# Four graph layers on one core: operands in PSUM, index arrays kept in SBUF, scans over eight features, gathers moved across stage ends, products on pairs of node tiles

## The reference

```
h = relu(layernorm(x)); x += segment_sum(h[src] * weight, dst) @ W0.T + b0
h = ...; per source node: sum, max and mean of edge_attr (32 features), and u
         x += relu([sum, max, mean, u] @ W1 + b1) @ W2 + b2
h = ...; hw[r] = h @ Wr[r] for 8 relations
         M = segment_sum(hw[etype, src] / degree[dst], dst)
         x += relu(0.2 h + 0.8 M)            (h where the degree is 0)
h = ...; e = leaky_relu(h[src] @ al + h[dst] @ ar); a = softmax of e over each dst
         x += elu(segment_sum(h[src] * a, dst))
```

## Time and profile before

| | us |
|---|---|
| device time, median of 3 runs | 24807.4 |
| lowest, highest | 24771.12, 24842.9 |
| span of the profiled execution | 21400.8 |
| POOL busy in the span | 16823.9 (79%) |
| DVE busy | 8437.1 (39%) |
| PE busy | 4183.5 (20%) |
| ACT busy | 2199.2 (10%) |

### The profile page before, as it was taken

The page is one execution under the profiler, slowest core; times in us unless marked ns, Lnnn a source line. Parts: engine busy times, 40 slices in busy tenths (PEclk is TensorE's granted clock), DMA queues, the critical chain, the costliest instruction groups (busy, mean ns, idle before and its releaser), DMA issues. The chain is left out here.

```text
span 21400.8 us, 135402 instructions
## 1 busy us (share of the span) xinstructions
PE 4183.5 (20%) x27708; PEld 3439.5 (16%) x27708; DVE 8437.1 (39%) x31691; ACT 2199.2 (10%) x10623; POOL 16823.9 (79%) x13464
## 2 busy tenths in 40 slices
PE   1111677777760000000061000000000000000000
PEld 1111566656650000000040000000000000000000
DVE  5555666666655455454431111111113222222223
ACT  0000444444440000000010000000000000000000
POOL 7888777777778888888856777777777787787777
PEclk9999755555555555555555555555555555555555
DMA  2111111111102222222221111111112111111112
GB/s 52 36 33 36 33 27 27 27 27 27 27 24 74 67 69 74 66 69 74 66 64 53 45 45 45 45 45 45 46 47 32 46 46 46 46 46 46 42 46 46
DMA packets 660027, 993.34 MB, mean 46 GB/s; under 512 B 393615, under 2 KB 447856, under 8 KB 629104
## 3 DMA queue, kind: packets, MB, share of 16 engines
q0 software_dynamic: 430432, 388.76, 9.6%
q10 hardware_dynamic: 28944, 432.98, 4.9%
q1 hardware_dynamic: 200192, 167.64, 2.9%
HBM read 466.94 MB, written 521.52 MB: 46 GB/s over the span
## 5 line engine op out<-in xcount | busy, mean ns | idle before, releaser
L338 POOL DMA_INDIRECT att_G<-att_table,att_idx x3240 | 3909.3, 1207 | 988.9 <-issue 986.9
L338 POOL DMA_INDIRECT rel_G<-rel_table,rel_idx x3240 | 3726.7, 1150 | 1203.7 <-issue 986.8
L338 POOL DMA_INDIRECT wsum_G<-h_table,wsum_idx x2160 | 3725.8, 1725 | 751.0 <-issue 732.2
L606 POOL DMA_INDIRECT by_src<-sort_row,sort_place_i x3240 | 3139.7, 969 | 987.4 <-issue 987.4
L448 DVE TENSOR_TENSOR_SCAN rel_S<-rel_same,rel_S,rel_G 128x60 f32<-128x60 f32 x3456 | 823.6, 318 | 3901.5 <-DMA rel_G<-rel_table,rel_idx 3901.5
L747 PE MATMUL pG<-sort_counts,sort_lowTf 128*128 128x98 f32 x6484 | 2211.3, 442 | 0.0
L338 POOL DMA_INDIRECT ahead_rows<-h_table,wsum_idx x1020 | 1773.6, 1739 | 310.8 <-issue 310.8
L492 PE MATMUL wsum_C<-wsum_high,wsum_low 128*128 128x98 bf16 x6480 | 568.5, 283 | 5788.6 <-DVE wsum_high L368 5788.6
L747 PEld LDWEIGHTS pG<-sort_counts,sort_lowTf 128*128 128x128 f32 x6484 | 1692.7, 319 | 0.0
L426 DVE TENSOR_TENSOR_SCAN att_er<-att_same,att_er,att_er_in 128x60 f32<-128x60 f32 x54 | 18.5, 342 | 3719.3 <-DMA att_G<-att_table,att_idx 3719.3
L492 PEld LDWEIGHTS wsum_C<-wsum_high,wsum_low 128*128 128x128 bf16 x6480 | 522.1, 143 | 5834.9 <-DVE wsum_high L368 5834.9
(11 more groups left out here) (362 smaller groups left out, 11319.2 us busy)
## 6 DMA issues: line engine op xcount, KB each, us to landing
scan_att<-att_S ACTq DMA_DIRECT2D x54, 1980.0 KB, 7.2
scan_wsum<-wsum_S ACTq DMA_DIRECT2D x54, 1920.0 KB, 6.8
scan_pool<-pool_S ACTq DMA_DIRECT2D x36, 2880.0 KB
scan_rel<-rel_S ACTq DMA_DIRECT2D x54, 1920.0 KB, 6.8
pool_row<-by_src SPq DMA_DIRECT2D x36, 1485.0 KB
sort_feat<-in_attr SPq DMA_DIRECT2D x54, 960.0 KB
by_src<-sort_row,sort_place_i POOLq DMA_INDIRECT x3240
rel_G<-rel_table,rel_idx POOLq DMA_INDIRECT x3240
```

The costliest lines, as they stand in the source:

```text
L338: pool.indirect_dma_start(out=G[s][:, j, :], out_offset=None, in_=table, in_offset=bass.IndirectOffsetOnAxis(ap=idx[s][:, j:j + 1], axis=0 ...
L606: pool.indirect_dma_start(out=by_src, out_offset=bass.IndirectOffsetOnAxis(ap=place_i[s][:, j:j + 1], axis=0), in_=row[s][:, j, :], in_off ...
```

## The change

- **PSUM side operands.** `parts` (for the one-hots), the weights, the neighbour comparison and the small arrays of `att` are put into PSUM, so that most DVE instructions with two tensor inputs read one of them from there. The multiplication now writes to a new tile `Gf`.
- **Scans over eight features.** `Gf` and `Sf` are feature by edge column (64 by 60). One scan runs over 8 features by 60 columns (480 elements), with `wide`, 8 copies of the comparison, in PSUM. The element at each feature's first column carries the state: `wide` is 0 there, and one instruction puts the chunk before into `Gf` first. In `rel` ACT turns `G` into `Gf`; in `wsum` and `att` the DVE multiplication does. ACT turns `Sf` back into `S` before the store. `G[s]` is free once it is turned. `pool_side` does the same with 5 features by 90 columns, its result in the memory of `H`.
- **Resident index arrays.** `src`, `dst` and the weights are loaded once in the first stage; `rel_index` once at the start of `rel`, `er_start` once at the start of `att`. ACT copies 60 columns of indices per chunk to `idx`.
- **Gathers across stages.** POOL gathers chunk 18 at the end of the first `wsum` stage and chunk 19 at the start of the scatter; the fetch of `V_pool` (into `H`) moves from the start of `first_layers` to the end of the second `wsum` stage. `places` becomes part of both `wsum` stages.
- **Pairs of node tiles.** In `first_layers` PE transposes two tiles of 64 features at a time (4 transposes a group instead of 7), and the products use weights padded with zeros to 128 rows.
- **`X`** is not kept through the first stages but loaded again at the start of `first_layers`, ahead of that stage's other loads on SP's queue.

The core of the diff:

```diff
+        wt_all = sb("wt_all", [P, J], c=early)
+        def gather_lead(pool, s, chunk):
+            for j in range(chunk * L, (chunk + 1) * L):
+                pool.indirect_dma_start(out=lead["rows"][s][:, j - chunk * L, :], out_offset=None, in_=h_table,
+                                        in_offset=bass.IndirectOffsetOnAxis(ap=src_all[:, j:j + 1], axis=0)
+                                        ).then_inc(lead["gathered"][s], 16)
...
+                act.dma_start(src_all[:, 0:J], src).then_inc(s_types, 16)
+                act.dma_start(dst_all[:, 0:J], dst[0:EP].rearrange("(p j) -> p j", p=P)).then_inc(s_types, 16)
+                act.dma_start(wt_all[:], weight).then_inc(s_types, 16)
...
+                G = lead["rows"] if pooled else slots("G", [P, L, width])
+                Gf = sb(f"{NAME}_Gf", [P, D, L], F32, c)
+                Sf = sb(f"{NAME}_Sf", [P, D, L], F32, c)
+                wide = ps(f"{NAME}_wide", [P, 512], c=c)[:, 0:BY * L].rearrange("p (f j) -> p f j", f=BY)
...
-                    parts = sb(f"{NAME}_parts", [P, 2, SIDE], BF16, c)
+                    parts = ps(f"{NAME}_parts", [P, 512], c=c)[:, 0:2 * SIDE].rearrange("p (m j) -> p m j", m=2)
...
                     def gather(i, s):
-                        pool.wait_ge(loaded[s], 16 * NL * i + 16 * NL)
-                        pool.wait_ge(scanned, 2 * i + s + PRIMED - 1)
+                        pool.wait_ge(index_ready, 2 * i + s + 1)
+                        pool.wait_ge(turned, 2 * i + s + 1)
...
-                    if ahead:
-                        gather(0, 1)
-                    with pool.Fori(1 if ahead else 0, NC // 2) as i:
+                    with pool.Fori(1 if pooled else 0, NC // 2) as i:
                         for s in range(2):
                             gather(i, s)
+                    if counts and not pooled:
+                        gather_lead(pool, 0, c1)
+                    if pooled:
+                        pool.wait_ge(pstored, 16 + 32 * NC)
+                        pool.wait_ge(pstate_ready, NC + 1)
+                        fetch(pool, scan_pool, end_src, H, 1)
...
+                                v.tensor_tensor(wide[:, :, 1:L],
+                                                dst_all[:, bass.ds(at + 2, L - 1)].unsqueeze(1).to_broadcast([P, BY, L - 1]),
+                                                dst_all[:, bass.ds(at + 1, L - 1)].unsqueeze(1).to_broadcast([P, BY, L - 1]),
+                                                ALU.is_equal).then_inc(wide_ready, 1)
...
-                                v.tensor_tensor(G[s][:], G[s][:], wt[s][:].unsqueeze(2).to_broadcast([P, L, D]), ALU.mult).then_inc(weighed, 1)
+                                v.tensor_tensor(Gf[:], by_feature, wt_near[s].unsqueeze(1).to_broadcast([P, D, L]), ALU.mult).then_inc(turned, 1)
...
-                            for f in range(D):
-                                last = v.tensor_tensor_scan(S[s][:, :, f], keep, G[s][:, :, f], S[1 - s][:, L - 1, f:f + 1], ALU.mult, ALU.add)
+                            v.scalar_tensor_tensor(Gf[:, :, 0], Sf[:, :, L - 1], ex[s][:, 0, 0:1] if kind == "att" else keep_first[:, 0:1],
+                                                   Gf[:, :, 0], ALU.mult, ALU.add).then_inc(begun, 1)
...
+                            for f in range(0, D, BY):
+                                flat = lambda a: a.rearrange("p f j -> p (f j)")
+                                last = v.tensor_tensor_scan(flat(Sf[:, f:f + BY, :]), flat(wide), flat(Gf[:, f:f + BY, :]), 0.0,
+                                                            ALU.mult, ALU.add)
...
+                            if kind == "rel":
+                                act.wait_ge(gathered[s], 16 * L * (i + 1))
+                                act.wait_ge(scanned, k + PRIMED)
+                                nc.scalar.copy(Gf[:], G[s][:].rearrange("p j f -> p f j")).then_inc(turned, 1)
...
+                            nc.scalar.copy(S[s][:, :, 0:D].rearrange("p j f -> p f j"), Sf[:]).then_inc(taken_out, 1)
...
+                    for n in range(NPC):
+                        sp.dma_start(X[:, n * TP:(n + 1) * TP, :],
+                                     x.rearrange("(h p) d -> p h d", p=P)[:, n * TP:(n + 1) * TP, :]).then_inc(s_w, 16)
                     pooled.load(sp)
...
-                    fetch(pool, scan_pool, end_src, VP, 1)
                     fetch(pool, scan_wsum, end_dst, V, 0)
...
+                    def turn_pairs(rows):
+                        for i, t in enumerate(pair_starts):
+                            last = nc.tensor.transpose(pV[:, i * P:(i + 1) * P], rows[:, t:t + 2, :].rearrange("p t d -> p (t d)"), ident[:])
...
-                            mm(pW[k % 2][:], HTt[n % 2][:, t * P:(t + 1) * P], wr[:].rearrange("d r f -> d (r f)"),
+                            pair, half = in_pair[t]
+                            mm(pW[k % 2][:], HTt[n % 2][:, pair * P:(pair + 1) * P], wr[:, half].rearrange("d r f -> d (r f)"),
```

More of the change, by code:

```diff
@@ L540, in scatter_by_source @@
-        def scatter_by_source(ahead):
+                        pe.wait_ge(count_ready, 1)
+                        mm(within[:, 0:HT], below_b[:], count[:], start=True, stop=True)
+                        mm(total[:, 0:HT], ones[:], count[:], start=True, stop=True).then_inc(prefix_ready, 1)
+        def scatter_by_source(lead_chunk):
             AHEAD = 4
@@ L614, in _ @@
                         pool.sem_inc(rows_used, 1)
[L615 to L620 removed]
+                    gather_lead(pool, 1, lead_chunk)
                     issue(0, 0, None)
```

432 lines of the change are left out of this document (246 added, 186 removed).

## The result

| | before | after |
|---|---|---|
| median of 4 runs, us | 24,811.55 | 23,636.11 |
| ratio (95% interval) | | 0.952 (0.951 to 0.954) |
| profiled run: time, span | not given, 21,400.8 | 23,605.72, 23,604.0 |

The change is faster by 1175 us where I forecast 3862. The time lies outside my range. So there are no 3407 us outside the span: the profiled execution whose rows stand ahead of the prediction was a shorter one than any that was timed.

A forecast was written before the change was run, and what follows sets the result against it. POOL's gathers, stretched by DVE instructions with two large SBUF inputs, were taken as the bound. Removing the stretch -4012, remaining holds +40, stage ends +110: -3862 us, from 24,807 to 20,945 us, range 20,300 to 21,400.

The forecast's parts named there:

- 59 us: First `wsum`: DVE's work per chunk (one-hots 44, scans 8.9, multiplication 4.2, rest 2), below POOL's 74.9 us.
- POOL stays the bound: First `wsum`: POOL's 74.9 us a chunk still sets the pace, with DVE 16 us to spare.
- An undisturbed gather costs 1.249 us: All gather stages: 0.944 us plus a 0.305 us gap per gather; the excess, 4012 us together, goes.
- I keep them as a constant: Outside the stages: 3407 us between the profiled span and the median of the runs stay unchanged.
- The hold as such: Gather stages: DVE instructions with two large SBUF inputs stretch POOL's gathers; PSUM operands end that, -4012 us.
- Sizes: DVE and ACT per chunk: multiplication 4.2 us, ACT's turns some 4 us each way, `wide` scan about 1.1 us.
- Stage ends: Between stages: +41 before the scatter, -40 at second `wsum`, +90 for the `V_pool` fetch, in all +110 us.
- the outside part scales: Whole kernel: unprofiled runs are slower in proportion, by 1.159, so the time is 20,330 us; chance 0.15.
- The hold stays: Gather stages: POOL still held despite a PSUM operand, freed only by shorter scans; 23,690 us, chance 0.04.

The follow-up runs named there:

- e3: The changed kernel with the one-hots' operand `parts` back in SBUF, as in the kernel before: 22,709.01 us.
- e6: e3 with the scans' mask `wide` of `rel` and `att` also back in SBUF instead of PSUM: 22,661.51 us.
- e11: e3 with each gather of `rel` moving 16 rows instead of 128, the other 112 left out: `rel` takes 4506.2 us.
- e0: The kernel before, unchanged, profiled again: time 24,822.76 us, span 24,820.7 us.

## Why the prediction was wrong, point by point

- **The chunk of `wsum`: "59 us", "POOL stays the bound".** This is the step that failed. The sum took each chunk at POOL's 74.9 us, with DVE's 59 us beside it, and put PE, with its products and its hand-overs, at nothing. Beside gathers without holds PE takes longest, one product in 2.80 us, and a chunk takes 2134 / 18 = 119 us in the first stage and 3587 / 34 = 106 in the second. Forecast -802 and -1694, measured -10 and -744: 1742 of the 2645 us by which the span fell short of the forecast (3862 - 1217). What POOL gained in the first stage it waited for at the next chunk; e3 shows that taking the hold back gives 1000 us.
- **"An undisturbed gather costs 1.249 us".** The second step that failed. It is true of POOL's own time, not of what a long run of gathers can do: 1.391 (e6, e11). For `rel` and `att` that alone is 2 x (4507 - 4047) = 920 us. The sum had -667 and -849, measured are -154 and -484, 878 us less; both stages now stand at the floor.
- **"I keep them as a constant".** This came out nearly right, but by luck. A gap of 3407 us between a span and the runs was a sign that the profiled execution was of another kind. 3004 of them lie inside the scatter stage (7131 us in e0, not 4127), which the change left as it was (-15), so they stood in both kernels as the sum had them. The gather stages of e0 are within 100 us of those in the earlier trace rows. What the short execution did was to hide the two failed steps: all its groups of 30 products took 2.63 us, and its 3240 scatters went at 1.274 us each. Why that one execution lacked the slow hand-overs stays open: none of the later ones did. All later ones were recorded as well, so no run shows whether an unrecorded execution has them.
- **The hold as such** was right in mechanism: `wsum`'s gathers went from 4 to 18 us to a mean of 944 ns, and e3 brings 2.83 and 3.77 back with the one operand. The Trainium skill (SBUF — State Buffer, "Who interferes with whom") infers that a `tensor_tensor` does not hold up descriptor writing; e3's rows disagree, as the earlier trace rows did. For the wide scans e6 finds a hold of one scan at most. In `rel` the hold was worth less than the prediction read from the earlier trace rows: in e0 the mean gather there is 1.005 us, so holds make up some 200 us, while POOL waits 616 us for keys (217 in the earlier trace rows), as I read it because the 64 short scans before them are late.
- **Sizes.** The wide scan 1.134 us (forecast 1.11). The turning multiplication 6.65 us, not 4.2: the Trainium skill's 1.7 to 2.5 ns a column (Vector Engine (DVE) Microarchitecture Reference, "Measured stream behaviour on trn2") fits, 6.65 / 3840 = 1.73 ns. ACT's turns 6.66 to 7.39 us, not 4. In `rel` none of these was on the path. In the first `wsum` the multiplication and ACT's turn are part of POOL's wait of 49 us, 5 us more of it than by the forecast sizes.
- **Stage ends.** Before the scatter +167, not +41: the last chunk but one is made beside the stage's last gathers and those of chunk 18, and DVE waits 73 and 58 us between its one-hots. Start of the second `wsum` +56, not -40. On to `rel` -43 where I had +98 (+90 for the fetch, +8 at the start of `rel`); this I haven't taken apart.
- **The rivals.** That the outside part scales came nearest in kind (the execution isn't typical) and went the wrong way; its price was a gain. *The hold stays* had the price 23,690, 54 us from the median, and that is chance: the holds of `wsum` went, as its mean gather of 944 ns shows, and other waits took their place. No rival had a floor under the gathers or a slowed PE.

## What to carry to other kernels

When a profile's span and the measured time differ by more than a few microseconds, first find a profile that doesn't, and cost the change on that. An engine that is freed of a wait can slow those it had left in peace: after each such edit ask what its extra work runs beside, and try each operand by itself (here one of them cost 1000 us while the rest of the change gained 2200, by e3). For an engine that issues many small indirect DMAs, look for the floor per DMA, in a stage where it waits for nothing and over several chunks. And put every engine of a stage into the sum, the ones far from the bound too.

## What the runs showed that I had not expected

- An indirect DMA costs 1.391 us in a long run of them, the same for 128 rows and for 16 (4506.4, 4506.2 us for 3240), though POOL issues one in 1.249 or 1.14. Sixty with a pause behind them go at 1.249 (first `wsum`).
- While they run, the other engines get an instruction through only every 0.7 to 1.4 us (PE one weight load and one product in 2.80 us), even with no semaphore between, and PE for some 5 us after the last of them. 0.70 and 1.40 are the half and the whole of the 1.400 at which the gathers of `rel` settle; why is open.
- Beside 60 fills on POOL the tiles of the scatter stage run on at 67 us a chunk, beside 60 indirect DMAs at 132.
- Long instructions are little touched: eight wide scans in a row took 8.49 us beside the gathers. The 64 short ones of the kernel before took 15.25 us in the short execution, but in e0's `rel` 61 us a chunk at the median and up to 81, most of it idle time between them. The changed kernel's scans beside gathers, and e0's group:

```profile
15061.66 8.49 DVE L520 TENSOR_TENSOR_SCAN rel_Sf<-rel_wide,rel_Gf 128x480 f32<-128x480 f32 x8
```

```profile
L448 DVE TENSOR_TENSOR_SCAN rel_S<-rel_same,rel_S,rel_G 128x60 f32<-128x60 f32 x3456 | 1051.0, 341 | 3580.5 <-issue 2129.7
```
